# A four-layer convolution kernel: last layer with overlap-add, gelu and product moved ahead of the transposes, and border columns moved by DMA

## The chip, the cores and the metric

One core of a Trainium2 chip runs the whole program. The metric is the device time of one execution in microseconds. Names of engines are those of the profile: PE (TensorE matmul), PEld (its weight loads), DVE, ACT, POOL (GpSimd), and SP, whose queue issues DMAs.

## The reference

The input `x` is [4, 48, 256, 256], float32. Four residual layers follow, `x = x + conv_i(groupnorm(x))`. The change touches only the last one:

```
y = einsum('oc,bchw->bohw', w_in, x)                  # 48 -> 288 channels
f = rfft2(8x8 patches of y) * fft_mask;  y = irfft2(f)
y = depthwise 3x3 convolution of y, zero padding
x1, x2 = split(y, 2, axis=channels)                   # 144 and 144
out = einsum('oc,bchw->bohw', w_out, gelu(x1) * x2)   # 144 -> 48
```

## The kernel before, in words

The last layer is `stage_l3` (lines 2104 to 2548). It works on **slabs** of 8 image rows: 33 bands times 2 pairs of images, 66 slabs, numbered n. In a slab there are 64 patches of 8x8 pixels: 32 across, in two images. The 288 channels are handled in three groups j of 96, and u = 3n + j counts groups.

For each slab, PE does the following, and this order is written out by hand:

- `channels` (L2268): the 48 to 288 mixing, into `y` with 64 pixels on the partitions. ACT and DVE copy it out of PSUM (`read_y`, L2370) in 12 pieces.
- `convolve` (L2292), for each j: per channel one matmul of the 64 patches with a 64x100 matrix `d` that holds mask and 3x3 convolution together. It gives 10x10 outputs for each 8x8 patch: the outer ring belongs to the neighbouring patches. ACT and DVE copy the result to `turn` (`read_turn`, L2378) in five pieces each, with **patches on the partitions**.
- `transpose` (L2318): 50 transposes of 128x112, which put **channels on the partitions**. ACT (8) and DVE (5) copy them from PSUM to `spread` (L2403, L2391).
- On POOL, `join` (L2523, L2525) adds the columns that two neighbouring patches share; L2539 adds the bottom rows saved from the band above in `strip`; L2547 saves the new bottom rows. Neighbouring patches lie side by side in the free dimension of `spread`, so this is plain addition.
- `gelu` on ACT (L2415) and the product on DVE (`gated`, L2473), four pieces for each j; then `project` (L2333), 24 matmuls of 48x48 by 512 columns per slab on PE, and `residual` (L2482) on DVE.

SP loads `x` for the next slab (L2211, two of 48 partitions; L2213, two rows of ones with one partition each), stores the result (L2219) and loads the residual (L2228, eight). Another stage matters for the reading: L813 loads inputs of the first layer with 49 partitions each.

Semaphores order all this. Each engine works through its own list in order, so a wait holds up all that stands behind it.

Of the kernel before, what the change touches and what calls it, by code (L numbers as in the profile page):

```python
# [20 lines left out]
R = 8  # L21
# [48 lines left out]
def l3_channels():  # L70

    return [g * 3 * C + j * C + r * (C // 2) + i for r in range(2) for j in range(3) for g in range(2) for i in range(C // 2)]


def l3_place(pos):

    pair, x, parity = pos // 20, pos % 20 // 2, pos % 2
    return 2 * pair + parity, x
# [92 lines left out]
def lay_out(i):  # L171
# [79 lines left out]
    order = l3_channels()  # L251
    d["l3_win"] = np.ascontiguousarray(i["L3_conv_w_in"].T[:, order])
    real, pairs = _pairs()
    fm = i["L3_conv_fft_mask"].reshape(C6, 8, 5)[order]
# [8 lines left out]
    d["l3_dwb"] = np.repeat(np.ascontiguousarray(i["L3_conv_w_dw"].reshape(C6, 9)[order].T)[None], 64, axis=0)  # L263
    wout = np.zeros((HI + C, 3, C), np.float32)
    for s in range(2):
        wout[s * HI:s * HI + C] = i["L3_conv_w_out"].T.reshape(3, C, C).transpose(1, 0, 2)
    d["l3_wout"] = wout
# [1836 lines left out]
def stage_l3(nc, D, S):  # L2104
# [3 lines left out]
    BANDS = H // 8 + 1  # L2108
    CH = C // 2
# [7 lines left out]
    TILES = PPOS // 2  # L2117
    TS = 4
    TG = -(-TILES // TS)
    ON_DVE = (1, 4, 6, 9, 11)  # L2120
    TURNS = [[i for i in range(TG) if (i in ON_DVE) == bool(k)] for k in range(2)]
    E = [len(groups) for groups in TURNS]
    PAIRS = 5
    HN = 512
    LANES = HI + C
    with nc.cleanup_on_exit(), ExitStack() as ctx:
# [10 lines left out]
        turn = sb("turn", [128, PPOS, HI])  # L2137
        spread = sb("spread", [LANES, PAIRS, 10, 4, TX])
        strip = sb("strip", [LANES, 3, 8, 4 * TX])
        x = sb("x", [HI + C + 1, TX, PX])  # L2140
        gate, spare = sb("gate", [LANES, 3, 8 * W]), sb("spare", [LANES, 2 * HN])
        out = sb("out", [LANES, 2, 2, HN])
        win = spare[0:C, 0:C6]
        lt, wy = sb("lt", [C, 2, HI + C + 1]), sb("wy", [HI + C + 1, 2, C6])
        wout = sb("wout", [LANES, 3, C])
# [3 lines left out]
        MIX_SLOTS, CONV_SLOTS = (3, 2, 0, 1), (0, 1, 2, 0, 1)  # L2149
        consts, prep, wy_done, wy_out, cleared = (sem(n) for n in ("consts", "prep", "wy_done", "wy_out", "cleared"))  # L2150
        d_in = [sem(f"d_in{j}") for j in range(3)]
        x_loaded, res_loaded, stored = sem("x_loaded"), sem("res_loaded"), sem("stored")
        a_done, a_out, b_done, b_out = sem("a_done"), sem("a_out"), sem("b_done"), sem("b_out")
        e_done, e_out = [sem("e_done0"), sem("e_done1")], [sem("e_out0"), sem("e_out1")]
        f_done, f_out = [sem("f_done0"), sem("f_done1")], sem("f_out")
        joined, added, saved = sem("joined"), sem("added"), sem("saved")
        mixing, saving, blank = sem("mixing"), sem("saving"), sem("blank")
# [3 lines left out]
        def inner(pair):  # L2161

            return spread[:, pair, 1:9, :, :].rearrange("p x g t -> p x (g t)")

        def one_half(part, pair):

            return inner(pair)[:, :, part * 2 * TX:(part + 1) * 2 * TX]

        def turned(u, i):

            k = int(i in ON_DVE)
            return k, u * E[k] + TURNS[k].index(i) + 1

        def turned_up_to(u, i):

            return [u * E[k] + sum(g <= i for g in TURNS[k]) for k in range(2)]

        def pieces_of(i):

            return min((min(TS * i + TS, TILES) - 1) // 10 + 1, 4)  # L2180

        def flat_piece(n, j, piece):

            if j == 0 and piece >= 2 and n % 2 == 1:
                return spare[:, (piece - 2) * HN:(piece - 1) * HN]
            return gate[:, j, piece * HN:(piece + 1) * HN]

        def band_piece(n, j, piece):

            return flat_piece(n, j, piece).rearrange("p (x m) -> p x m", x=8)  # L2190

        def slabs(work):

            for q in range(2):
                for ty in range(BANDS):
                    n = q * BANDS + ty
                    work(q, ty, n, n == 0, n == 2 * BANDS - 1)

        @block.sync
        def _(sp):  # L2200
# [3 lines left out]
            def load_x(q, ty, n, first):  # L2204
# [3 lines left out]
                for s in range(2):  # L2208
                    at = B * NBLK if isinstance(ty, int) and ty == BANDS - 1 else ty + (q + 2 * s) * NBLK
# [5 lines left out]

            def store(n):
                sp.wait_ge(f_out, n * 4)
                for side in range(2):
                    sp.dma_start(D["out"][n - 1, side], out[side * HI:side * HI + C].rearrange("p s k n -> p (s k n)"))\  # L2219
                      .then_inc(stored, 16)  # L2220

            def load_residual(q, ty, n, first):
                if not first:
                    sp.wait_ge(stored, n * 32)
                for s in range(2):
                    for p in range(4):
                        src = D["x3"][q + 2 * s, :, ty * 8 + 2 * p:ty * 8 + 2 * p + 2, 1:W + 1]
                        sp.dma_start(out[p % 2 * HI:p % 2 * HI + C, :, p // 2, s * W:(s + 1) * W], src)\  # L2228
                          .then_inc(res_loaded, 16)
# [7 lines left out]
            def slab(q, ty, n, first, last):  # L2237
                if not last:
                    nq, nty = (1, 0) if q == 0 and isinstance(ty, int) and ty == BANDS - 1 else (q, ty + 1)
# [359 lines left out]
```

## Time and profile before

| | us |
|---|---|
| median of 3 runs (lowest, highest) | 12443.44 (12438.75, 12449.53) |
| span of the profiled execution | 12461.3 |
| of it, from the last layer's first convolution matmul to its last | 9449.7 to 12429.4 |
| PE busy, whole span | 12084.7 |

The profiled execution gives no other time of its own than its span, which is 0.14% above the median. A span runs from the first to the last instruction. Busy time of PE is that of overlapping matmuls. Windows and chain are given in microseconds from the start of the span.

### The profile page before, as it was taken

The page shows a single profiled execution, that of the slowest core. Times are in us where ns is not written, and L with a number is a line of the kernel's source. Part 1 is how long each engine was busy: PE and PEld are TensorE (multiplying, and loading weights), DVE is VectorE, ACT ScalarE, POOL GpSimd, SP SyncE. Part 2 cuts the span into 40 slices and gives each one's busy share as a digit, 9 for nine tenths or more (in the row PEclk, how much of TensorE's full clock was granted, in tenths as well). Part 3 has the DMA queues.
Part 4 walks back from the last instruction along what each step waited for, and adds up shares of the span by engine and source line. Part 5 has one row for each costly group of instructions (what it writes and reads, how often), then busy time and mean ns, then how long its engine had stood idle before and what let it go on. Part 6 is the DMA issues. An engine that isn't in the chain of part 4 may idle for free. (4 is left out here: it accounts for less than half of the span.)

```text
span 12461.3 us, 389987 instructions
## 1 busy us (share of the span) xinstructions
PE 12084.7 (97%) x160850; PEld 8648.5 (69%) x160850; DVE 7757.3 (62%) x17493; ACT 5633.1 (45%) x11858; POOL 4999.7 (40%) x4364
## 2 busy tenths in 40 slices
PE   8999999899989999899999999999998999999999
PEld 7877444499977777555555555555557888888887
DVE  0000455444435545788888888888887777777777
ACT  0000111243433333455555555555556777777776
POOL 0000222212420055566666666666663444444444
PEclk9999999999999999999999999999999999999999
DMA  4333465695984587766666666666662222222222
GB/s 142 132 132 132 127 159 154 147 179 89 166 164 146 147 230 199 93 88 87 88 89 88 88 88 88 88 88 87 89 87 67 57 57 57 57 54 56 55 55 52
DMA packets 2289545, 1323.30 MB, mean 106 GB/s; under 512 B 1876085, under 2 KB 2199164, under 8 KB 2202256
## 3 DMA queue, kind: packets, MB, share of 16 engines
q1 hardware_dynamic: 2013196, 1200.80, 49.5%
q10 hardware_dynamic: 275072, 105.14, 3.7%
q8 instruction: 843, 13.81, 0.5%
q14 instruction: 434, 3.55, 0.1%
HBM read 648.82 MB, written 450.45 MB: 88 GB/s over the span
## 5 line engine op out<-in xcount | busy, mean ns | idle before, releaser
L1803 PE MATMUL l_m<-l_wa,l_pix 128*128 128x288 f32 x8192 | 2211.4, 413 | 2.7 <-DVE l_wb L1985 2.7
L1803 PEld LDWEIGHTS l_m<-l_wa,l_pix 128*128 128x128 f32 x8192 | 1475.5, 190 | 688.8 <-issue 361.9
L1659 POOL TENSOR_TENSOR l_qkv<-l_qkv,l_copies 128x576 f32<-128x576 f32 x1024 | 1437.1, 1403 | 631.3 <-DVE l_qkv L1996 621.5
L1649 POOL TENSOR_TENSOR l_pix<-l_raw 128x516 f32<-128x516 f32 x1024 | 1217.1, 1189 | 1042.6 <-DVE l_t L2033 1017.1
L1484 PE MATMUL l1h_ps<-l1h_ring,l1h_w 96*96 96x256 f32 x6120 | 1328.8, 379 | 62.7 <-ACT l1h_ring L1426 60.2
L1484 PEld LDWEIGHTS l1h_ps<-l1h_ring,l1h_w 96*96 96x96 f32 x6120 | 999.8, 163 | 391.5 <-issue 60.4
L2318 PEld LDWEIGHTS l_e<-k_ident,l_turn 128*112 128x112 f32 x9900 | 1069.1, 133 | 173.0 <-issue 110.6
L2318 PE MATMUL l_e<-k_ident,l_turn 128*112 128x128 f32 x9900 | 1158.2, 275 | 11.4 <-ACT l_turn L2403 3.0
L2403 ACT ACTIVATE l_spread<-l_e 112x512 f32<-112x512 f32 (+1 forms) x1584 | 871.7, 569 | 521.4 <-PE l_e L2318 509.5
L1517 DVE SCALAR_TENSOR_TENSOR l1h_ring<-l1h_ps,l1h_bias,l1h_columns 96x256 f32<-96x256 f32 x1020 | 670.4, 657 | 678.4 <-PE l1h_ps L1484 672.7
L517 PE MATMUL l0a_rows<-l0a_x 128*49 128x245 f32 x8144 | 1043.0, 371 | 0.0
L878 PE MATMUL l0b_bank<-l0b_x,l0b_w 49*64 49x512 f32 x9216 | 1000.5, 592 | 4.4 <-DVE l0b_w L904 4.4
L2391 DVE COPY l_spread<-l_e 112x512 f32<-112x512 f32 x990 | 683.8, 691 | 354.8 <-PE l_e L2318 351.3
L1898 ACT ACTIVATE l_ks<-l_f 94x384 f32<-94x384 f32 x1024 | 497.9, 486 | 843.2 <-PE l_f L1818 843.2
L1818 PE MATMUL l_f<-l_qkv,l_a 64*94 64x384 f32 x4096 | 834.8, 483 | 1.6 <-POOL l_qkv L1659 1.5
L878 PEld LDWEIGHTS l0b_bank<-l0b_x,l0b_w 49*64 49x64 f32 x9216 | 431.1, 133 | 570.9 <-issue 570.9
L1809 PE MATMUL l_m<-l_wb,l_left 58*128 58x288 f32 x4096 | 774.5, 455 | 0.0
L1468 POOL TENSOR_TENSOR l1h_columns<-l1h_blocks,l1h_ring 96x2048 f32<-96x2048 f32 x63 | 350.7, 5588 | 1035.9 <-DVE l1h_ring L1517 1035.9
L2292 PE MATMUL l_a<-l_d,l_y 64*64 64x100 f32 x15048 | 741.3, 248 | 8.3 <-issue 7.2
L2292 PE MATMUL l_b<-l_d,l_y 64*64 64x100 f32 x15048 | 743.6, 248 | 3.7 <-issue 3.2
L1903 ACT ACTIVATE l_sd<-l_mv,l_eps 128x4 f32<-128x4 f32 x512 | 152.3, 297 | 1286.7 <-DVE l_mv L2016 1286.7
L1909 ACT ACTIVATE l_y<-l_i,l_shift,l_rsd 128x96 f32<-128x96 f32 x2048 | 709.3, 427 | 14.4 <-DVE l_shift L2023 0.4
(269 smaller groups left out, 22947.3 us busy)
## 6 DMA issues: line engine op xcount, KB each, us to landing
l0a_x<-x_px_dram SPq DMA_DIRECT2D x128, 1176.0 KB, 5.1
l0b_x<-x_in_dram SPq DMA_DIRECT2D x128, 493.8 KB
l_raw<-l_raw SPq DMA_DIRECT2D x128, 483.6 KB, 7.3
l_raw<-x_dram SPq DMA_DIRECT2D x1270, 48.0 KB, 3.7
l_x<-x3p_dram SPq DMA_DIRECT2D x132, 384.0 KB
l_out<-x_dram SPq DMA_DIRECT2D x528, 96.0 KB, 2.4
out_dram<-l_out SPq DMA_DIRECT2D x132, 384.0 KB, 4.5
x_dram<-l0b_out ACTq DMA_DIRECT2D x256, 193.5 KB, 3.1
```

The source lines that it names most:

```text
L517: last = nc.tensor.matmul(o[odd * ODD:odd * ODD + C1, lo:lo + n * C1], x[:, ks, ys, 2 + odd, :], x[:, k, y, e0 + odd:e0 + odd + n, :].rear ...
L878: last = nc.tensor.matmul(bank[2 * n + rt][h * HI:(h + 1) * HI, :], w[part, t, :], rows(part, k, 4 * n + h + t // 3 - rt)[:, :, t % 3:t % ...
L1484: last = nc.tensor.matmul(ps[g][0:C2, 0:GI * V], w[:, kernel, s, :], ring[:, g, before % DEEP, :, s:s + V], start=(s == 0), stop=(s == 2))
L1649: nc.gpsimd.tensor_tensor(pix[:, n % 2, i, half * HALF:(half + 1) * HALF].rearrange("p (r w) -> p r w", w=PW), in0, in1, op).then_inc(pix_ ...
L1659: nc.gpsimd.tensor_tensor(q, q, copies[:, g % 2, 1:2, :].broadcast_to([128, 2, OUTC]), ALU.add)\
L1803: last = nc.tensor.matmul(bank[i][:, 0:OUTC], pix[:, k, i, first:first + 128], wa[:, b, i, :], start=True, stop=(i in (1, 2)))
L1809: nc.tensor.matmul(bank[i][:, 0:OUTC], left[rows, k, first:first + 128], wb[rows, b, :], start=False, stop=True).then_inc(conv_done, 1)
L1818: last = nc.tensor.matmul(f[0:SLOTS, h, 0:2 * QK].rearrange("p (n o) -> p n o", n=2), a[k, 0:SLOTS], qkv[k, j % 4, 2 * r:2 * r + 2, 0:QK], ...
L1909: last = nc.scalar.activation(y[:, g, m, :], iv[:, m * C2:(m + 1) * C2], ACT.Identity, scale=rsd[:, g, m:m + 1], bias=shift[:, g, m:m + 1])
L2292: last = nc.tensor.matmul(bank[part * 64:(part + 1) * 64, i * PPOS:(i + 1) * PPOS], y[k, c, :], d[k, c, :], start=True, stop=True, skip_gr ...
L2318: last = nc.tensor.transpose(e[i % 4][0:LANES, at:at + 128], flat[:, q * 128:q * 128 + LANES], S["k_ident"][:])
L2403: return nc.scalar.activation(o, i, ACT.Copy)
```

## The change

Only `stage_l3`, and the layout of its constants and output, change.

- The channels are paired so that `x1` and `x2` of the same channel stand in the same partition of `turn`, which is now [128, 2 buffers, 10 x, 10 y, 2, 24]. The 128 partitions are two halves of channels, times two images, times 32 patches. Each group of 32 partitions is one row of patches.
- Columns that neighbouring patches share now lie on neighbouring partitions. `move_edges` on SP brings them together: eight DMAs for each j, from `turn` to `edge`, each of 31 partitions and 480 floats (1920 bytes) a partition. The edge add, the carry from `strip` and the saving of the strip then run on POOL with partitions as they are (960, 768 and 768 elements).
- Gelu and the product work on `turn` in two halves of 768 elements, before the transposes.
- The transposes take `gate`: 16 of 128x128 for each j instead of 50 of 128x112. ACT alone copies them out, four copies of 512 (`read_rows`) instead of 13 by ACT and DVE.
- The projection is 48 matmuls with 24 rows each, on four row groups of PE and into four banks, instead of 24 with 48 rows.
- The order on PE becomes: convolve 0, transpose 2 of the slab before, convolve 1, project the slab before, transpose 0, convolve 2, channels of the next slab, transpose 1. The residual comes in four loads instead of eight.

The core of the diff, lines added and kept:

```diff
+    return pos % 10, pos // 10
...
+        turn = sb("turn", [128, 2, 10, 10, 2, CH])
+        edge = sb("edge", [128, 2, 2, EDGE])
+        strip = sb("strip", [128, 3, 8, 2 * C])
...
+        gate = sb("gate", [128, 2, PX, LANE])
+        rows = sb("rows", [128, 3, GROUPS, 2, 2 * TX])
...
+        CONV_SLOTS = ((1, 2, 3, 1, 2), (1, 2, 0, 1, 0), (2, 3, 0, 1, 2))
+        TURN_SLOTS = ((1, 0), (3, 0), (0, 3))
...
+            def move_edges(n, j):
+
+                u = n * 3 + j
+                sp.wait_ge(a_out, conv_at(n, j, COMP))
+                sp.wait_ge(b_out, conv_at(n, j, COMP))
+                if u >= 2:
+                    sp.wait_ge(edged, u - 1)
+                for first in range(0, 128, TX):
+                    here, there = slice(first, first + TX - 1), slice(first + 1, first + TX)
+                    for side, column, dst, src in ((0, 9, there, here), (1, 0, here, there)):
+                        sp.dma_start(edge[dst, u % 2, side, :],
+                                     turn[src, u % 2, column].rearrange("p y g i -> p (y g i)")).then_inc(edge_in[u % 2], 16)
...
             def slab(q, ty, n, first, last):
                 if not last:
+                    load_x(*((1, 0) if q == 0 and ty == BANDS - 1 else (q, ty + 1)), n + 1, False)
+                move_edges(n, 0)
+                move_edges(n, 1)
                 if not first:
+                    store(n - 1)
+                move_edges(n, 2)
...
+            def transpose(n, j, ended):
+
                 u = n * 3 + j
+                for i, bank in enumerate(turn_banks(j)):
+                    if j == 0 and i % 2 == 0:
+                        bank_pair_read(conv_at(n, 1, 4 + i // 2))
+                    elif j == 1 and i % 2 == 0:
+                        bank_pair_read(conv_at(n, 2, 2 + i // 2) if ended else (n + 1) * AB + 9 + i // 2)
+                    elif j == 2 and i == 0 and ended:
+                        pe.wait_ge(t_out, u * 4)
+                    elif j == 2 and i == 2 and not ended:
+                        bank_pair_read(conv_at(n + 1, 0, 3))
+                    if i % 2 == 0:
+                        pe.wait_ge(gate_out, u * 2 + 1 + i // 2)
+                    for k in range(4):
+                        group = 4 * i + k
+                        last = nc.tensor.transpose(bank[:, k * 128:(k + 1) * 128],
+                                                   gate[:, u % 2, 4 * group:4 * group + 4, :].rearrange("p m i -> p (m i)"),
                                                    S["k_ident"][:])
+                    last.then_inc(t_done, 1)
...
+            def project(n, ended):
+
+                pe.wait_ge(t_out, n * 12 + 12)
+                bank_pair_read(conv_at(n, 2, 5) if ended else conv_at(n + 1, 1, 2))
+                for k in range(6):
+                    j, r = k // 2, k % 2
+                    for m in range(4):
+                        lanes = slice(m * LANE, m * LANE + CH)
+                        for side in range(2):
+                            last = nc.tensor.matmul(e[m][side * HI:side * HI + C, :], wout[lanes, j, r, :],
+                                                    rows[lanes, j, side * 8:(side + 1) * 8, r, :], start=(k == 0), stop=(k == 5),
                                                     skip_group_check=True)
+                        if k == 5:
+                            last.then_inc(p_done, 1)
...
+                    if j == 0 and not first:
+                        transpose(n - 1, 2, False)
+                    if j == 1:
+                        if not first:
+                            project(n - 1, False)
+                        transpose(n, 0, False)
+                if not last:
+                    channels(1 if q == 0 and ty == BANDS - 1 else q, n + 1, False)
+                transpose(n, 1, last)
...
+            if g == 0 and u >= 2:
+                eng.wait_ge(gate_out, 2 * u - 2)
+                eng.wait_ge(saved, u - 1)
+            eng.wait_ge(done, conv_at(n, j, g) + 1)
+            places = turn[:, u % 2].rearrange("p x y g i -> p (x y) g i")
+            copy(places[:, :, part, CSTARTS[g]:CSTARTS[g] + CSIZES[g]],
+                 slots[CONV_SLOTS[j][g]][part][:, 0:CSIZES[g] * PPOS].rearrange("p (c t) -> p t c", t=PPOS)).then_inc(ready, 1)
...
+            def gelu(u, h):
+
+                if h == 0:
+                    act.wait_ge(edged, u + 1)
+                    act.wait_ge(carried, u + 1)
+                nc.scalar.activation(half(u, 0, h), half(u, 0, h), ACT.Gelu).then_inc(gelu_out, 1)
+
+            def read_rows(n, j):
 
                 u = n * 3 + j
+                if j == 0 and n > 0:
+                    act.wait_ge(p_done, n * 4)
+                for i, bank in enumerate(turn_banks(j)):
+                    act.wait_ge(t_done, u * 4 + i + 1)
+                    copy(rows[:, j, 4 * i:4 * i + 4].rearrange("p q r t -> p (q r t)"), bank[:]).then_inc(t_out, 1)
...
+                u = n * 3
+                for g in range(COMP):
+                    read_turn(act, copy, 0, n, 0, g, a_done, a_out)
+                    if g in (0, 2) and not first:
+                        gelu(u - 1, g // 2)
+                if not first:
+                    read_rows(n - 1, 2)
+                for g in range(COMP):
+                    read_turn(act, copy, 0, n, 1, g, a_done, a_out)
+                for h in range(2):
+                    gelu(u, h)
+                read_rows(n, 0)
+                for g in range(COMP):
+                    read_turn(act, copy, 0, n, 2, g, a_done, a_out)
+                if last:
+                    for h in range(2):
+                        gelu(u + 1, h)
+                else:
+                    for g in range(YR):
+                        read_y(act, copy, 0, n + 1, g, False, a_done, b_done, a_out)
+                        if g in (3, 6):
+                            gelu(u + 1, g // 6)
+                read_rows(n, 1)
...
+            def gated(u, h):
+
+                dve.wait_ge(gelu_out, u * 2 + h + 1)
+                if u >= 2:
+                    dve.wait_ge(t_done, u * 4 - 6 + 2 * h)
+                nc.vector.tensor_tensor(gated_half(u, h), half(u, 0, h), half(u, 1, h), ALU.mult).then_inc(gate_out, 1)
+
+            def residual(n, m):
+
+                dve.wait_ge(p_done, n * 4 + m + 1)
+                if m == 0:
+                    dve.wait_ge(res_loaded, n * 64 + 64)
+                o = out[:].rearrange("p y s (t x m) -> p y x (s t) m", x=2, m=4)[:, :, :, :, m]
+                nc.vector.tensor_tensor(o, e[m][0:HI + C, :].rearrange("p (y x t) -> p y x t", y=4, x=2), o, ALU.add)\
...
+                for g in range(COMP):
+                    read_turn(dve, nc.vector.tensor_copy, 1, n, 0, g, b_done, b_out)
+                    if g in (1, 3) and not first:
+                        gated(u - 1, g // 2)
+                for g in range(COMP):
+                    read_turn(dve, nc.vector.tensor_copy, 1, n, 1, g, b_done, b_out)
+                for h in range(2):
+                    gated(u, h)
+                if not first:
+                    for m in range(4):
+                        residual(n - 1, m)
+                for g in range(COMP):
+                    read_turn(dve, nc.vector.tensor_copy, 1, n, 2, g, b_done, b_out)
+                if last:
+                    for h in range(2):
+                        gated(u + 1, h)
+                else:
+                    for g in range(YR):
+                        read_y(dve, nc.vector.tensor_copy, 1, n + 1, g, False, b_done, a_done, b_out)
+                        if g in (4, 7):
+                            gated(u + 1, g // 7)
...
+                    tile = turn[:, u % 2].rearrange("p x y g i -> p x (y g i)")
+                    pool.wait_ge(a_out, conv_at(n, j, COMP))
+                    pool.wait_ge(b_out, conv_at(n, j, COMP))
+                    pool.wait_ge(edge_in[u % 2], 128 * (u // 2) + 128)
+                    nc.gpsimd.tensor_tensor(tile[:, 1:9:7], tile[:, 1:9:7], edge[:, u % 2], ALU.add).then_inc(edged, 1)
+                    pool.wait_ge(edged, u + 1)
                     if ty == 0:
+                        pool.sem_inc(carried, 1)
                     else:
                         pool.wait_ge(saved, u - 2)
+                        nc.gpsimd.tensor_tensor(tile[:, 1:9, 0:2 * C], tile[:, 1:9, 0:2 * C], strip[:, j], ALU.add)\
+                            .then_inc(carried, 1)
+                    pool.wait_ge(carried, u + 1)
+                    pool.sem_inc(mixing, 1)
+                    nc.gpsimd.tensor_copy(strip[:, j], tile[:, 1:9, 8 * C:10 * C]).then_inc(saved, 1)
```

## Rows read from the trace of the kernel before

**Rows 1.** The page: busy time by engine, and the granted clock in 40 slices.
```profile
PE 12084.7 (97%) x160850; PEld 8648.5 (69%) x160850; DVE 7757.3 (62%) x17493; ACT 5633.1 (45%) x11858; POOL 4999.7 (40%) x4364
...
PEclk9999999999999999999999999999999999999999
```

**Rows 2.** One line, L2292: its matmuls' min/median/max, first and last start.
```profile
L2292 PE MATMUL l_a<-l_d,l_y x15048: 242/246/426, 9449.7 to 12429.4; 64*64 64x100 f32 x198
```

**Rows 3.** Window of steady slabs: us; PE, PEld, DVE, ACT, POOL busy; clock, DMA share, GB/s.
```profile
9900.00:12400.00 2500.00, 2441.47 (x56770) 2123.42 (x56762) 1959.21 (x3198) 1867.11 (x3476) 1065.15 (x990) 1.00 0.25 56
```

**Rows 4.** Chain of work inside one slab: start us, us, what.
```profile
11001.40 5.74 PE l_e L2318 x50
...
11011.61 2.60 PE l_e L2333 x21
...
11020.27 0.23 PE l_a L2292
...
11024.55 1.47 PE l_e L2268 x48
...
11032.85 5.60 PE l_e L2318 x50
```

**Rows 5.** Groups by line and shape, last stage: count, busy us, mean ns, idle before.
```profile
L2318 PE MATMUL l_e<-k_ident,l_turn 128*112 128x128 f32 x9900 | 1158.2, 275 | 11.4 <-ACT l_turn L2403 3.0 <-DVE l_turn L2378 0.8 <-ACT l_y L2403 0.3
...
L2403 ACT ACTIVATE l_spread<-l_e 112x512 f32<-112x512 f32 x1386 | 796.0, 596 | 509.5 <-PE l_e L2318 508.8 <-issue 0.5
...
L2473 DVE TENSOR_TENSOR l_gate<-l_gate,l_spread 112x512 f32<-112x512 f32 x726 | 474.0, 684 | 4.1 <-ACT l_gate L2415 3.4
L2539 POOL TENSOR_TENSOR l_spread<-l_spread,l_strip 112x1024 f32<-112x1024 f32 x192 | 453.6, 2363 | 15.1
L2415 ACT ACTIVATE l_gate<-l_spread 112x512 f32<-112x512 f32 x726 | 421.2, 625 | 2.0 <-POOL l_spread L2525 1.1 <-POOL l_spread L2539 0.9
L2378 DVE COPY l_turn<-l_b 128x500 f32<-128x500 f32 x594 | 402.9, 678 | 135.6 <-PE l_b L2292 120.1
L2403 ACT ACTIVATE l_turn<-l_a 128x500 f32<-128x500 f32 x594 | 392.4, 661 | 149.9 <-PE l_a L2292 132.0
```

**Rows 6.** Waits of the last stage: engine and line, for whom, us, times, longest.
```profile
ACT l_spread L2403 <- PE l_e L2318: 509.5, 986, 2.5
```

**Rows 7.** The DMA-issuing queue SP through one slab: start us, us, line, count.
```profile
11021.09 4.57 SPq L2228 DMA_DIRECT2D l_out<-x_dram  x8
11032.93 0.31 SPq L2211 DMA_DIRECT2D l_x<-x3p_dram  x1
...
11078.00 0.31 SPq L2211 DMA_DIRECT2D l_x<-x3p_dram  x1
```

**Rows 8.** DMA view, 11033 to 11040 us: packets, and what was issued.
```profile
DMA packets 135, 0.84 MB, mean 121 GB/s; under 512 B 34, under 2 KB 34, under 8 KB 34
...
q1 hardware_dynamic: 132, 0.80, 57.9%
...
l_x<-x3p_dram SPq DMA_DIRECT2D x2, 384.0 KB
l_x<-k_ones_dram SPq DMA_DIRECT2D x2, 8.0 KB
```

**Rows 9.** SP's issues, 1338 to 1345 us, where loads have 49 partitions.
```profile
1338.20 1.98 SPq L813 DMA_DIRECT2D l0b_x<-x_in_dram  x4
```

**Rows 10.** DMA view, 1338 to 1345 us.
```profile
DMA packets 97, 0.93 MB, mean 132 GB/s; under 512 B 7, under 2 KB 7, under 8 KB 7
```

**Rows 11.** Windows: loads with 49 partitions; 1 KB loads; 1 KB copies within SBUF.
```profile
1342.00:1344.00 2.00, 2.00 (x11) 2.00 (x11) 0.00 (x0) 0.00 (x0) 0.06 (x1) 0.50 0.46 175
11022.00:11024.00 2.00, 2.00 (x104) 2.00 (x100) 1.74 (x4) 1.91 (x5) 1.13 (x2) 1.00 0.78 199
8200.40:8202.40 2.00, 2.00 (x14) 1.29 (x14) 1.09 (x5) 1.35 (x4) 0.44 (x2) 1.00 0.82 174
```

**Rows 12.** Line L2228: from issue to landing.
```profile
DMA to landing us min/median/max: 2.0/2.4/11.3
```

More of the change, by code:

```diff
@@ L262, in lay_out @@
     d["l3_m"] = m
[L263 to L267, printed above, removed]
+    d["l3_dwb"] = np.repeat(np.ascontiguousarray(i["L3_conv_w_dw"].reshape(C6, 9).T)[None], 64, axis=0)
+    wout = np.zeros((4, 32, 3, 2, C), np.float32)
+    wout[:, 0:C // 2] = i["L3_conv_w_out"].T.reshape(3, 2, C // 2, C).transpose(2, 0, 1, 3)
+    d["l3_wout"] = wout.reshape(128, 3, 2, C)
     return d
@@ L2116, in stage_l3 @@
     AB = YR + 3 * COMP
[L2117 to L2125, printed above, removed]
+    EDGE = 10 * C
+    LANE = 32
+    GROUPS = PX // 4
     with nc.cleanup_on_exit(), ExitStack() as ctx:
@@ L2351, in slab @@
                     convolve(n, j)
-                    if j < 2 and not first:
-                        project(n, j)
-                    if j == 2 and not last:
-                        nq = 1 if q == 0 and isinstance(ty, int) and ty == BANDS - 1 else q
-                        channels(nq, n + 1, False)
-                    transpose(n, j, first)
-            slabs(slab)
-            for part in range(2):
-                project(2 * BANDS, part)
-        def read_y(eng, copy, s, n, first, done, other, ready, between):
-            for g, size in enumerate(SIZES):
-                if g == 0 and not first:
-                    eng.wait_ge(other, n * AB)
-                eng.wait_ge(done, n * AB + (g + 1))
-                bank = slots[MIX_SLOTS[g % 4]][s]
-                m0 = s * TX + STARTS[g]
-                copy(y[:, :, m0:m0 + size], bank[:, 0:size * C3].rearrange("p (t c) -> p c t", c=C3)).then_inc(ready, 1)
-                between(g)
@@ new lines, in slab, with read_y @@
+                transpose(n, 1, last)
+            slabs(slab)
+            transpose(N - 1, 2, True)
+            project(N - 1, True)
+        def read_y(eng, copy, s, n, g, first, done, other, ready):
+            if g == 0 and not first:
+                eng.wait_ge(other, n * AB)
+            eng.wait_ge(done, n * AB + (g + 1))
+            bank = slots[MIX_SLOTS[g % 4]][s]
+            m0 = s * TX + STARTS[g]
+            copy(y[:, :, m0:m0 + SIZES[g]], bank[:, 0:SIZES[g] * C3].rearrange("p (t c) -> p c t", c=C3)).then_inc(ready, 1)
@@ L2476, in residual @@
-            def residual(n, part, s):
-                dve.wait_ge(f_done[s], n * 2 + (part - 1))
-                if part == 0 and s == 0:
-                    dve.wait_ge(res_loaded, n * 128)
-                o = out[:, s, part, :].rearrange("p (m x) -> p m x", x=8)
-                nc.vector.tensor_tensor(o, e[2 + s][0:LANES, :].rearrange("p (x m) -> p m x", x=8), o, ALU.add)\
+            dve.wait_ge(blank, 1)
+            dve.sem_inc(blank, 1)
+            for g in range(YR):
+                read_y(dve, nc.vector.tensor_copy, 1, 0, g, True, b_done, a_done, b_out)
```

308 lines of the change are left out of this document (85 added, 223 removed).

## The prediction, made before the changed kernel ran

> **What bounds the kernel now.** I began with the page: PE is busy 97% of the span at full clock [rows 1]. Then I took the last layer alone. The convolution line runs from 9449.7 to 12429.4 us [rows 2], so 66 slabs take 45.2 us each, and SP's loads repeat at the same pace, 11032.93 and 11078.00 [rows 7]. In steady slabs PE is busy 2441 of 2500 us, DVE 1959, ACT 1867, POOL 1065, and the DMA engines 25% at 56 GB/s [rows 3]. The chain of work says who ends last: it is PE's list, one piece after another [rows 4]. ACT stands idle 509.5 us in this stage for transposes [rows 6]. So a slab is bound by PE, and its pieces can be read off the chain: one convolution of a group 4.3 us (11020.27 to 11024.55), the channels 8.3 (to 11032.85), one set of 50 transposes 5.75, half a projection 2.6 [rows 4]. Together 3 x 4.3 + 8.3 + 3 x 5.75 + 2 x 2.6 = 43.6 us, with 1.6 us of waits.
>
> **PE after the change.** A transpose costs 5.75 / 50 = 0.115 us. 48 in place of 150 take 5.5 us and save 11.7. The wider tile (128 columns for 112) streams the same 128 columns, so I keep 0.115. Convolutions and channels keep their count. The projection doubles to 48 matmuls of half the rows. Before, 24 matmuls (48 instructions, since float32 takes two each) took 5.2 us, so four ran at once at 0.43 us a round [rows 4]. No row shows row groups of 32 at work. The bounds are eight at once (5.2 us) and one at a time (96 x 0.43 = 41 us). The nearest row ran four tiles at once on separate parts of the array. I take 5.2, and 10.4 for four at once is covered by what follows. PE needs 12.9 + 8.3 + 5.5 + 5.2 = 31.9 us a slab.
>
> **ACT, DVE, POOL.** ACT loses its copies to `spread` (8 of each 13) and takes 12 copies of 512 at 0.6 us; gelu in 6 pieces of 768 elements, scaled from 625 ns for 512 [rows 5], is 0.9 us each. In sum about 28 us. DVE loses its share of the 13 copies and makes 6 products of 768 elements, 1.0 us each by 684 ns for 512 [rows 5]; about 25 us. POOL's two-input add costs 2363 / 1024 = 2.3 ns an element [rows 5]: edge add (960) 2.2 us, carry (768) 1.8 us, and saving under 1 us, three times, about 15 us. None of them would bound the slab; all that is removed from them is hidden either way.
>
> **What is added: the border columns.** This is the part on which the time hangs. `move_edges` issues 8 DMAs for each group, 24 a slab, on SP. SP's issues take 0.3 to 0.57 us each [rows 7], so 3 to 5 us for a group. That is bearable. The question is how fast the data moves. Each DMA has 31 partitions of 1920 bytes.
>
> The packet counts say how a DMA is spread. From 11033 to 11040 us SP issued two DMAs of 48 partitions and two of one. The queue shows 132 packets: 34 small ones, and 98 others, one for each partition. The 34 are completions: 2 x 16 + 2 x 1 [rows 8]. So 48 partitions go to 16 engines, and one partition to one engine. With 49 partitions, four loads were queued within 2 us [rows 9]; the one that finished by 1345 us left 7 completions [rows 10]. While all four were pending the DMA engines were busy 0.46 of 16, thus about seven, at 175 GB/s [rows 11]. Two things follow. 49 partitions did not go to 16 engines but to 7, which divides 49, as 16 divides 48. And four loads in flight together did not fill other engines: they sat **on the same seven**. 31 has no divisor but 1 and itself. So each of the 8 DMAs should run on one engine, and all on the same one, one after another.
>
> The Trainium skill, "DMA: Bandwidth & Descriptors", section "Why a DMA increments its semaphore by 16 and not by 1", says so: the largest number up to 16 that divides both sides' outermost dimension, 127 partitions giving 1, and the lowest-numbered engines. By that rule the sum is the one below; by sixteen engines it would be that of the first rival.
>
> What one engine gives: 175 / 7 = 25 GB/s for packets of 10 KB. With 1 KB packets on all engines it was 199 / (0.78 x 16) = 16 GB/s, and for copies within SBUF 174 / (0.82 x 16) = 13 GB/s [rows 11]. 59.5 KB therefore take between 2.4 and 4.5 us. I take **2.55 us**, near the low end, because a lone engine has no fifteen others to contend with. A group's 8 DMAs take 20.4 us on that engine (bounds 19 and 36), a slab's 24 take 61.2. The store of 96 rows of 8 KB gives this engine 6 packets at 25 GB/s, 2.0 us, and it is queued in between.
>
> **Can the engine be kept busy all the time?** Two buffers of `turn` let group 1 be queued while group 0 moves, and group 2 is ready in time: after group 0 lands come POOL 4.0, gelu 1.8, product 1.0, residual 2.7, convolve and read 4.5, 14 us, under 20. But ACT and DVE work in order. At the start of a slab they read piece 0 of group 0, then stop for the gelu of the last slab's group 2, and only then read the rest, for which `move_edges` waits. So once a slab the engine runs dry. From landing to next packet: POOL 2.2 + 1.8, gelu 0.9, two reads 1.4, gelu 0.9, product 1.0, last read 0.6, and the fixed part of a DMA 1.9 (2.4 us to landing less the transfer itself [rows 12]): 10.8 us. The loads of `x` and of the residual pass in this gap and cost nothing. PE's 31.9 us lie beside the DMAs. At 1.2 GHz, as granted at 1342 us [rows 11], they would be 64 us and still mostly beside them.
>
> **Sum.** 61.2 + 2.0 + 10.8 = 74.0 us a slab against 45.2: 28.8 x 66 = 1901 us more. The profiled execution's span of 12461 would become 14362; it stands 18 us (0.14%) above the median of the runs, so the median is 12443 + 1901 = **14345 us**. Setup (three more fills on DVE, a few us) and the tail are under 30 us together.
>
> **Rivals.**
>
> *The columns spread over the engines.* If the 31 partitions were dealt out unevenly over 16 engines, or successive DMAs took different engines, a group's columns would arrive 5 to 6.5 us after its last read. Then PE bounds the slab again. Its waits: after convolve 0, gelu of group 0 can start after reads 2.3, DMAs 6, POOL 4.0, about 12.5 us; PE has convolve 1, projection and transposes (11.4 us) for that, then waits for gelu and product, and convolve 2 waits for two residual adds. About 5 us of waits give 37 us a slab, 8.2 x 66 = 541 us less: **11,900 us**, faster. Against it: 49 partitions went to seven engines and stayed there [rows 10, 11]. The point that decides: with 2.0 + 10.8 us beside it, the slab is even at (45.2 - 12.8) / 3 = 10.8 us a group, 1.35 us a DMA, which two engines would give. Chance 0.12.
>
> *The engine is one, and slow.* If 1920-byte copies within SBUF go at 13 to 16 GB/s as in [rows 11], a group takes 30 to 36 us and a slab 103 to 121: 16,200 to 17,400 us. For it: those are the rows with the nearest packet size. Against: sixteen engines shared the ports there. Chance 0.06.
>
> *The projection goes one matmul at a time.* 41 us instead of 5.2. It stands ahead of transpose 0 and thus of convolve 2, whose columns come 14 us late for the idle engine: 88 us a slab, 15,300 us. Against: four tiles ran at once before [rows 4]. Chance 0.04. The Trainium skill, "TensorEngine Tiling (Array Packing)", section "Tiling Modes", lists 32x64 as eight tiles; no run here shows it.
>
> **How the numbers follow.** One engine at 2.3 to 3.3 us a DMA, the forecast, holds 0.78: 68 to 92 us a slab, 13,900 to 15,500 us. The slower cases bring 0.10 and the spread case 0.12. Range 13,600 to 15,900: this takes in the forecast with a faster engine (2.2 us, 66 us a slab) and the projection's case, and leaves out the spread case and the slowest engine. A measurement of this kernel tells about 0.2% from no change. All cases but the spread one are slower: slower 0.87, faster 0.12; for "within 0.2%" a DMA would have to take 1.35 us exactly: 0.01.
>
> **What the changed kernel's profile would show.** Right: DMA share near 1/16 plus the loads, about 0.15, in the last layer; 24 issues of 60 KB a slab that land 20 us and more after their issue; POOL's edge add waiting for them; completions of one packet a DMA; PE busy under half. Wrong: completions of 16 a DMA, landing in 2 to 4 us, PE above 80%. If the slab is longer and the transposes' and projection's matmuls stand close together, the time of one DMA is what I mis-sized; if the projection's row is far above 5 us, it is the row groups. If the engine turns out to have no gap, the once-a-slab stop costs less than 10.8 us.

## The result, and the profile after

The changed kernel takes **14431.67 us** (median of 4 runs, 14429.67 to 14436.68) against 12446.49 us (4 runs): ratio 1.160, 95% interval 1.158 to 1.161. The forecast was 14345 us. The difference of 1985 us (1974 between the spans of the profiled executions) lies in the last layer. From the first to the last start of the convolution line (9454.2 to 14380.1), divided by 66 as in [rows 2], a slab takes 4925.9 / 66 = 74.6 us, where 74.0 was forecast; that is 29.5 us a slab more than before, 1946 us in all. The work behind the last convolution is 23 us longer, and the first one starts 4.5 us later. Slab lengths below are all taken that way.

The page of the changed kernel (busy time, granted clock, and the head of the chain that ended last) answers to [rows 1]:

```profile
PE 11788.2 (82%) x157286; PEld 8331.2 (58%) x157286; DVE 7087.2 (49%) x16108; ACT 5164.2 (36%) x10670; POOL 4680.8 (32%) x3770
...
PEclk9999999999999999999999999977777777777777
...
DMA 14%; SPq 9%; POOL 4%; PE 3%; DVE 3%; issue 1%; ACT 1%; POOLq 0%; ACTq 0%; DVEq 0%
```

PE is no longer what ends the stage: the chain runs through the DMAs and SP's queue. Steady slabs, with the columns of [rows 3] (PE, PEld, DVE, ACT, POOL busy; clock, DMA share, GB/s):

```profile
9900.00:14200.00 4300.00, 2279.59 (x55681) 1922.52 (x55681) 1446.51 (x2114) 1518.06 (x2574) 826.63 (x513) 0.74 0.20 52
```

PE is busy 53% of the time, at a mean clock of 0.74. The waits of the stage name what comes last (engine and line, for whom: total us, times, longest):

```profile
POOL l_turn L2518 <- DMA l_edge<-l_turn: 3768.8, 182, 60.5
DVE l_gate L2469 <- ACT l_turn L2394: 2564.0, 197, 21.2
ACT l_turn L2394 <- POOL l_turn L2524: 2457.7, 192, 19.7
...
PE l_a L2318 <- DVE l_gate L2469: 1081.3, 67, 20.7
```

They are one wait handed on: POOL waits for the columns, ACT's gelu for POOL, DVE's product for the gelu, and PE's transposes for the product. How the columns travel is seen in 10 us with little else to move. The DMA view and the window of the same stretch:

```profile
DMA packets 118, 0.26 MB, mean 26 GB/s; under 512 B 5, under 2 KB 112, under 8 KB 112
```
```profile
11530.00:11540.00 10.00, 6.99 (x171) 6.43 (x164) 5.91 (x11) 5.48 (x11) 4.86 (x3) 0.86 0.07 26
```

112 packets are under 2 KB, 5 of them completions: 107 carry columns, which is 3.5 DMAs of 31. The other six are five rows of the store and one of PE's or another engine's instructions. All together move at 26 GB/s and with a DMA share of 0.07, just over 1/16: one engine, always busy. The 5 completions fit one for each DMA that ends, four for the columns and one for this engine's part of the store. Eight DMAs at 26 GB/s take 8 x 59.5 / 26 = 18.3 us. The edge adds of POOL, each of which waits for the eight DMAs of its group, show how long they take (the first three are those of groups 0, 1 and 2 of one slab, the last that of group 0 of the next):

```profile
11511.57 2.20 POOL L2518 TENSOR_TENSOR l_turn<-l_turn,l_edge 128x960 f32<-128x960 f32 x1 [25.37 <-DMA l_edge<-l_turn]
...
11530.60 2.23 POOL L2518 TENSOR_TENSOR l_turn<-l_turn,l_edge 128x960 f32<-128x960 f32 x1 [13.96 <-DMA l_edge<-l_turn]
...
11556.62 2.20 POOL L2518 TENSOR_TENSOR l_turn<-l_turn,l_edge 128x960 f32<-128x960 f32 x1 [20.91 <-DMA l_edge<-l_turn]
...
11587.38 2.20 POOL L2518 TENSOR_TENSOR l_turn<-l_turn,l_edge 128x960 f32<-128x960 f32 x1 [25.69 <-DMA l_edge<-l_turn]
```

The three distances are 19.0, 26.0 and 30.8 us here, and 19.1, 25.8 and 30.4 us as means of 60 slabs. The first is that of eight DMAs with nothing between. SP's issues of these DMAs (count, min/median/max ns):

```profile
L2201 SPq DMA_DIRECT2D l_edge<-l_turn x1584: 561/2222/3446, 9462.2 to 14393.4; - x198
```

In the median an issue holds SP for 2.2 us, about as long as one of these DMAs takes to move. The first three or four of a group whose queue is empty take 0.56 to 0.60 us, the later ones wait: SP is held back by its own queue. The once-a-slab stop can be followed through the engines' timelines (start us, us, engine, what; in brackets the idle time before and who ended it):

```profile
11556.62 2.20 POOL L2518 TENSOR_TENSOR l_turn<-l_turn,l_edge 128x960 f32<-128x960 f32 x1 [20.91 <-DMA l_edge<-l_turn]
11558.90 1.80 POOL L2524 TENSOR_TENSOR l_turn<-l_turn,l_strip 128x768 f32<-128x768 f32 x1
...
11560.79 0.84 ACT L2394 ACTIVATE l_turn<-l_turn 128x768 f32<-128x768 f32 x1 [14.85 <-POOL l_turn L2524]
11561.54 1.18 ACT L2387 ACTIVATE l_turn<-l_e 128x500 f32<-128x500 f32 x2
11562.59 0.84 ACT L2394 ACTIVATE l_turn<-l_turn 128x768 f32<-128x768 f32 x1
...
11563.72 0.95 DVE L2469 TENSOR_TENSOR l_gate<-l_turn 128x768 f32<-128x768 f32 x1
11564.58 0.57 DVE L2381 COPY l_turn<-l_e 128x400 f32<-128x400 f32 x1
...
11565.53 29.85 SPq L2201 DMA_DIRECT2D l_edge<-l_turn  x16
```
```profile
11562.00:11564.00 2.00, 1.75 (x33) 1.52 (x34) 2.00 (x4) 2.00 (x5) 0.00 (x0) 0.50 0.00 0
```

The columns of the last slab's group 2 land at 11556.6. From there POOL, gelu, reads, gelu, product, last read follow one another, and SP issues again at 11565.5. In between no column moves: until 11560.7 the engine passes its part of the loads of the residual and of `x` (48 packets of 1 KB and 8 of 8 KB), and then nothing (second fence, share 0.00 at 0 GB/s). Then the groups that stand for the steps of the forecast, by shape (count, busy us, mean ns, idle before; as in [rows 5]):

```profile
L2518 POOL TENSOR_TENSOR l_turn<-l_turn,l_edge 128x960 f32<-128x960 f32 x198 | 438.0, 2212 | 3993.8 <-DMA l_edge<-l_turn 3768.8 <-DVE l_y L2371 167.9 <-ACT l_y L2387 57.1
L2469 DVE TENSOR_TENSOR l_gate<-l_turn 128x768 f32<-128x768 f32 x396 | 372.3, 954 | 2564.0 <-ACT l_turn L2394 2564.0
L2332 PE MATMUL l_e<-l_rows,l_wout 24*48 24x512 f32 x6336 | 356.8, 590 | 0.7 <-ACT l_rows L2387 0.7
L2394 ACT ACTIVATE l_turn<-l_turn 128x768 f32<-128x768 f32 x396 | 325.9, 839 | 2509.9 <-POOL l_turn L2524 2457.7 <-POOLq L2521 52.2
L2477 DVE TENSOR_TENSOR l_out<-l_e,l_out 112x512 f32<-112x512 f32 x264 | 269.1, 1094 | 9.0 <-PE l_e L2332 9.0
```

The projection's busy time is 356.8 / 66 = 5.4 us a slab.

### The profile page after: what moved, and what is told of

Read it like the earlier page. It is cut to its first block and busy times, and to the rows that moved or that the text cites. A ratio compares the mean times of both kernels' runs of the same rounds, so it can differ in the third digit from the quotient of the medians.

```text
span 14434.9 us, 377731 instructions
## 1 busy us (share of the span) xinstructions
PE 11788.2 (82%) x157286; PEld 8331.2 (58%) x157286; DVE 7087.2 (49%) x16108; ACT 5164.2 (36%) x10670; POOL 4680.8 (32%) x3770
## 5 line engine op out<-in xcount | busy, mean ns | idle before, releaser
L2518 POOL TENSOR_TENSOR l_turn<-l_turn,l_edge 128x960 f32<-128x960 f32 x198 | 438.0, 2212 | 3993.8 <-DMA l_edge<-l_turn 3768.8
L2469 DVE TENSOR_TENSOR l_gate<-l_turn 128x768 f32<-128x768 f32 x396 | 372.3, 954 | 2564.0 <-ACT l_turn L2394 2564.0
L2296 PE MATMUL l_e<-l_d,l_y 64*64 64x100 f32 x17424 | 524.1, 272 | 994.8 <-ACT l_turn L2387 973.6
L2394 ACT ACTIVATE l_turn<-l_turn 128x768 f32<-128x768 f32 x396 | 325.9, 839 | 2509.9 <-POOL l_turn L2524 2457.7
L2318 PE MATMUL l_a<-k_ident,l_gate 128*128 128x128 f32 x1056 | 265.9, 402 | 1081.3 <-DVE l_gate L2469 1081.3
L2296 PEld LDWEIGHTS l_e<-l_d,l_y 64*64 64x64 f32 x17424 | 459.7, 150 | 1036.4 <-ACT l_turn L2387 986.3
L2318 PEld LDWEIGHTS l_a<-k_ident,l_gate 128*128 128x128 f32 x1056 | 194.8, 211 | 1153.5 <-issue 1153.5
```

The lines of the kernel that those rows point to most:

```text
L2296: last = nc.tensor.matmul(bank[part * 64:(part + 1) * 64, i * PPOS:(i + 1) * PPOS], y[rows_of, c, :], d[rows_of, c, :], start=True, stop=True,
L2318: last = nc.tensor.transpose(bank[:, k * 128:(k + 1) * 128], gate[:, u % 2, 4 * group:4 * group + 4, :].rearrange("p m i -> p (m i)"), S[" ...
L2518: nc.gpsimd.tensor_tensor(tile[:, 1:9:7], tile[:, 1:9:7], edge[:, u % 2], ALU.add).then_inc(edged, 1)
```

## The experiments

Theory A is that of the forecast: a DMA of 31 partitions runs on one engine, always the same, and the slab is 24 of them, the store and the stop. Its rivals are that the size or the number of the copies is what costs, whatever engines they use, or that another part of the change (POOL, the projection, the slower clock) sets the time. A kernel for which no range is given was executed once. Each batch had the kernel before beside it, with medians of 12453.78, 12461.86 and 12449.19 us.

**Two DMAs for each one** (16 + 15 partitions; nothing left out):

```
-  here, there = slice(first, first + TX - 1), ...
+  for low, count in ((0, 16), (16, 15)):
+      here, there = slice(first + low, first + low + count), ...
```

> Each DMA of 31 partitions is cut into one of 16 and one of 15: same bytes, same result, 48 DMAs a slab instead of 24. One engine for a partition count without divisors (A): 16 and 15 partitions use 16 and 15 engines, the columns arrive some 6 us after the last read, the slab falls from 75 to 37-40 us, 11,900 to 12,100 us. Rival: SP's issuing of so many DMAs is what takes the time (B): with twice as many the slab grows, above 15,000 us. Rival: copies within SBUF are slow by their bytes, on however many engines (C): no change, 14,400.

Measured 13078.34 us (13066.25 to 13080.94), ratio to before 1.050 (1.048 to 1.051), slab 54.2 us. Twice the DMAs for the same bytes, and 1353 us less: it is the spread over engines, not count or bytes, that held the changed kernel. But the time stands 1000 us above what A gave, and SP's queue shows a large part of why (issues of the columns):

```profile
L2203 SPq DMA_DIRECT2D l_edge<-l_turn x3168: 538/816/2059, 9468.3 to 13047.1; - x198
```

The issues with 16 partitions take 0.56 to 0.60 us, those with 15 take 0.82 to 0.85. With what SP waits for in them, 48 a slab hold it for 36.6 us, and the residual's loads and the others stand behind them.

**One partition fewer, two fewer, and about half.** In the three kernels the slice is 30, 29 or 17 partitions in place of 31; the columns of the partitions left over are not moved:

```
-  here, there = slice(first, first + TX - 1), slice(first + 1, first + TX)
+  here, there = slice(first, first + 30), slice(first + 1, first + 31)
```

> Each DMA moves 30 of its 31 partitions (the seam between the last two patches of a row is left out). A: 30 divides into 15 engines, 11,850 to 12,050 us. B and C: 14,300 to 14,432, since 3% of the bytes are gone.

> 29 of 31 partitions (two seams left out), 29 has no divisor. A: still one engine, 24 x 2 packets of 0.078 us less a slab, 3.7 us x 66 = 250 us less than the changed kernel, about 14,190. C: like the run with 30. If any count below 31 spreads: 11,900.

> 17 of 31 partitions (14 seams of each row left out), one engine by A: 24 x 14 packets less, 26 us a slab, 48.5 us, about 12,700 us; the stop once a slab stays. If the time of one DMA were fixed and not by packet (rival D): 14,400.

Measured: 30 partitions 12586.40 us (slab 46.8), 29 partitions 14187.55 (71.0), 17 partitions 13164.14 (55.5). One partition fewer takes away 1845 us, and one fewer again gives 1601 back. No rival by size does that. 30 has the divisor 15; 29 has none. From 31 to 29 the kernel loses 244 us, or 3.7 us a slab, for 48 packets less: 77 ns a packet, 25 GB/s, the rate of [rows 11]. The DMA view of 30 partitions, over the 7 us in which eight are issued:

```profile
DMA packets 310, 0.49 MB, mean 70 GB/s; under 512 B 101, under 2 KB 298, under 8 KB 298
...
l_edge<-l_turn SPq DMA_DIRECT2D x8, 56.2 KB
```

101 small packets, where there was one for each DMA: 15 each for seven DMAs make 105, so 30 partitions go to fifteen engines. Two times of A are missed. With 30 partitions it gave 12,050 us at most and 12,586 came; what holds that kernel is the subject of the next runs. With 17 it gave 12,700. A slab has 24 DMAs of 17 x 0.077 = 1.3 us, 31.4 us, so 24.1 us are left where I had put 12.8 for store and stop. The edge adds of that kernel lie 10.4, 23.3 and 22.2 us apart. So the stop that came once a slab now comes twice, 17.7 us without columns together: group 1's columns are through before group 2's are ready.

**Four DMAs for each eight** (112 + 15 partitions across the patch rows; at three seams a group the wrong neighbour's column is added):

```
-  for first in range(0, 128, TX):
+  for low, count in ((0, 112), (112, 15)):
```

> Four DMAs a group instead of eight: 112 and 15 partitions for each side (16 and 15 engines). The six patches at the seams between rows of patches get a column of the wrong row; everything else is as in the changed kernel. The runs with 30 partitions and with 16 + 15 left a slab of 47 and 55 us instead of the 37 I had put down for spread columns. Theory: SP's issuing, 0.87 us a DMA, is the next limit: four issues less a group, 3.5 us off the chain from last read to gelu, 42 to 44 us a slab, 12,250 to 12,400. Rival: the rest of the slab (half clock, instruction fetch) is what holds it: 47 us, 12,590.

Measured 12402.98 us, slab 44.2: 2.6 us a slab under 30 partitions, for 12 issues fewer, at the edge of the forecast 42 to 44. It is faster than before (12461.86 beside it), by half a per cent.

**No columns at all** (SP moves none; POOL adds what the buffer holds):

> No border columns are moved (POOL adds zeros): leaves out the DMAs and their wait, all else in place. It gives the floor of the rest. Theory: last read to POOL's add took 9.1 us with 30 partitions; without it 37 to 40 us a slab, 11,900 to 12,100. Rival: if PE is stalled by something else (fetch of its instructions behind the loads of x and of the residual), 42 or more, above 12,200.

Measured 12228.93 us, slab 41.5, above the theory's range and at the rival's. My first rival had put the slab *with* spread columns at 37 us. Even without any of them it is 4.5 us longer, so something beside the columns was missing from that price. Nor is this time the floor that I took it for: a kernel further down moves the columns and is faster.

**Reads of the next group ahead of gelu and product** on ACT and DVE (nothing left out; both buffers serve):

```
-  if g in (0, 2) and not first:
-      gelu(u - 1, g // 2)
   if not first:
+      for h in range(2):
+          gelu(u - 1, h)
```

> The changed kernel, but ACT and DVE finish reading group 0 before they do gelu and product of the slab before, so the next columns can be queued before the last have landed. One engine with a stop once a slab (A): the 10.6 us in which the queue is dry go, the loads of x and of the residual (5 us of that engine) no longer hide in it: 68 to 70 us a slab, 13,950 to 14,100. If the stop is not what empties the queue: 14,432.

Measured 14006.69 us, slab 68.1: 425 us off, 6.4 us a slab, as expected. It is the stop, and most of it goes when group 0's copies no longer wait for the gelu of the slab before: of the three distances between edge adds only the third, which holds the stop, fell, from 30.4 to 23.7 us. POOL's wait for the DMAs fell with it (the waits of this kernel):

```profile
POOL l_turn L2519 <- DMA l_edge<-l_turn: 3304.9, 180, 61.1
```

**Merged, seams made zero, x loaded later.** This version leaves nothing out. POOL multiplies both sides of `edge` by a column that is 0 at the seams, and SP issues the loads of `x` behind the columns of group 0:

```
+  move_edges(n, 0)
   if not last:
       load_x(...)
-  move_edges(n, 0)
...
+  nc.gpsimd.tensor_scalar(edge[:, u % 2, side], edge[:, u % 2, side], seam[:, side:side + 1], None, ALU.mult)
```

> As the run with four DMAs, made right: POOL multiplies the moved columns by 0 at the seams (two one-input operations of 480 elements, 1.0 us a group), and the load of x stands behind the columns of group 0 instead of right behind the load of the residual, so that the two do not fill the DMA engines together. If SP's issuing and the fetch of PE's instructions behind those loads are the two limits: 38 to 41 us a slab, 12,050 to 12,200, faster than both kernels. If the load's place does nothing: 43 to 45, 12,330 to 12,450.

Measured 12346.41 us (12344.10 to 12360.01), ratio 0.991 (0.990 to 0.993), slab 43.3. Faster than both kernels, yet short of what I expected. The number lies where "the load's place does nothing" had put it, but the reason is another, the price of the mask:

```profile
L2525 POOL TENSOR_SCALAR l_edge<-l_edge,l_seam x396: 1476/1483/3084, 9463.5 to 12312.0; 128x480 f32<-128x480 f32 x198
```

1.48 us for 480 elements in the median and 1.68 in the mean, three times what I had assumed, twice in each group and ahead of the edge add. The next kernel differs from this one by the mask alone and has a slab of 40.0 us: the mask costs 3.3 us a slab.

**The load of x alone** (the kernel with four DMAs a group, and only `load_x` put behind group 0's columns; the seams as there):

> The run with four DMAs a group, with only the load of x put behind the columns of group 0 (columns at the seams as wrong as there). If PE's idle time without a releaser in the convolutions (some 4 us a slab there) is its instructions waiting behind the joined loads of the residual and of x: about half of it goes, 2 us a slab, 12,250 to 12,300 against 12,403. If those gaps have another cause: 12,380 to 12,420.

Measured 12126.95 us, slab 40.0: 4.2 us a slab less than with the load ahead, 2.6% under before, and below the range I gave. A load put later, which nobody waited for, was worth more than all 12 saved issues. The kernel is even 1.5 us a slab faster than the one without columns, in which the load of `x` still stands ahead. Where the gain came from is seen best in the kernel with 30 partitions. SP there issues the residual's loads and those of `x` back to back:

```profile
11510.76 2.12 SPq L2216 DMA_DIRECT2D l_out<-x_dram  x4
11512.98 0.38 SPq L2186 DMA_DIRECT2D l_x<-x3p_dram  x1
```
```profile
11515.00:11518.00 3.00, 2.25 (x108) 2.06 (x96) 1.75 (x3) 2.09 (x4) 2.46 (x2) 1.00 1.10 204
11518.00:11521.00 3.00, 0.00 (x0) 0.00 (x0) 1.15 (x2) 1.36 (x3) 0.00 (x0) 0.79 0.69 126
11521.00:11524.00 3.00, 1.05 (x24) 1.05 (x28) 0.00 (x0) 0.00 (x0) 0.00 (x0) 0.50 0.01 3
```
```profile
11522.95 0.42 PE L2296 MATMUL l_a<-l_d,l_y 64*64 64x100 f32 x1 [5.70 <-issue]
```

The DMA engines are full, and PE stops for 5.7 us in the middle of a convolution, "issue": no semaphore, no operand. It goes on at half the clock. The same wait in the kernel with four DMAs a group, and in this one, from 9900 to 12100 us:

```profile
PE l_e L2296 <- issue: 106.5, 37, 5.2
...
PE l_b L2296 <- issue: 31.0, 16, 5.0
...
PE l_a L2296 <- issue: 28.3, 15, 3.4
```
```profile
PE l_e L2296 <- issue: 33.8, 40, 2.4
...
PE l_b L2296 <- issue: 9.2, 21, 0.9
PE l_a L2296 <- issue: 7.5, 14, 1.4
```

165.8 us in 50 slabs became 50.5 us in 55: 2.4 us a slab less. The mean clock rose from 0.93 to 0.97. PE's busy time in these windows went from 36.1 to 34.7 us a slab and its idle time from 8.1 to 5.3, which is the whole 4.2. The columns themselves didn't come sooner: from SP's first issue of a group to the edge add it took 5.6, 5.3 and 5.7 us with the load ahead, and 5.8, 7.0 and 5.7 with it behind.

What arrives late is PE's own instructions. The page has a DMA queue of kind "instruction", whose packets have 16 KB. In the kernel with 30 partitions, the DMA view has none of them from 11511 to 11520 us, while the loads fill the engines, and one from 11520 to 11522:

```profile
q1 hardware_dynamic: 996, 1.63, 94.2%
```
```profile
q1 hardware_dynamic: 16, 0.02, 6.6%
q8 instruction: 1, 0.02, 4.8%
```

It ended at 11521.64, and PE went on at 11522.95. After 9900 us this kernel has 59 stops of over 1.5 us for "issue" ahead of a convolution matmul, and every one of them ended 1.2 to 1.8 us after such a packet; a moment taken at random lies there in 10% of cases. With four DMAs a group it was 52 of 52 stops, and with the load of `x` behind the columns only three stops were left. That the two loads together delay these packets is shown by that last number; how they share the DMA engines is not.

**The residual's layout alone** (no columns, as above; the residual is added in the order of `out`'s memory, so that sums stand in other places):

```
-  o = out[:].rearrange("p y s (t x m) -> p y x (s t) m", x=2, m=4)[:, :, :, :, m]
+  o = out[:, m].rearrange("p s w -> p (s w)")
```

> The run without border columns, and the residual add reads and writes its tiles straight through instead of with a stride of 8 floats (sums land in the wrong places of the output, same number of elements). Theory: the stride makes each of the four adds 1.09 us instead of 0.69, and they stand between the projection and the last convolution of a slab: 1.6 us a slab less, 12,120 against 12,229. If they are hidden: 12,229.

Measured 12111.79 us, slab 39.6, 1.9 us less, as expected. The residual's group in the kernel without columns and in this one, each from 9900 to 12100 us:

```profile
L2470 DVE TENSOR_TENSOR l_out<-l_e,l_out 112x512 f32<-112x512 f32 x208 | 212.1, 1088 | 0.0
```
```profile
L2470 DVE TENSOR_TENSOR l_out<-l_e,l_out 112x512 f32<-112x512 f32 x220 | 135.9, 675 | 0.0
```

**The mask on DVE** in place of POOL (nothing left out):

> The mended kernel, with the seam columns multiplied by 0 on DVE instead of POOL. On POOL these two operations took 2.9 us or more a group, where 1.0 was expected, on the path from the columns' landing to gelu. Theory: 2 to 3 us a slab less than mended, 12,150 to 12,230. Rival: DVE then waits for the columns with its other work behind it and gives it back: 12,350 or more.

Measured 12328.28 us (12323.83 to 12331.25), ratio 0.990 (0.988 to 0.992), slab 42.9: short of the expectation again, and not told apart from the version with the mask on POOL (0.991 of the kernel before beside it). DVE does each multiply in 0.46 us and not in 1.48, but the wait moved with the work. The waits from 9900 to 12200 us:

```profile
POOL l_turn L2536 <- DVE l_edge L2474: 1363.9, 143, 14.2
```

DVE takes the mask in its own order, behind products, residual adds and reads, and POOL waits for that instead.

## Why the prediction was right, and where it was not

**What bounds the kernel now, and PE after.** Right in substance: PE no longer sets the end, and POOL, gelu and product took 2.2, 0.84 and 0.95 us for 2.2, 0.9 and 1.0. PE was busy 53% and not under half, and the DMA share was 0.20 and not 0.15; the mean clock fell to 0.74. PE was busy for 39.5 us a slab where I had 31.9; the largest miss is the transposes, 9.6 us for 5.5, at the lower clock. The forecast had said that half clock would be hidden mostly, and since the waits are for the columns, it was. The projection took 5.4 us a slab against 5.2 for twice the matmuls. Of the rivals, "one matmul at a time" falls by that row.

**The border columns.** Right in mechanism and size, and shown: 29, 30 and 31 partitions tell the divisor from the size. The time of one DMA was put at 2.55 us; 31 packets of 77 ns give 2.4, and eight of them 19.1 where I had 20.4. The slow engine of the third case (30 to 36 us a group) falls: a lone engine moves packets of 1920 bytes at 26 GB/s, as fast as those of 10 KB.

**The loads beside the columns.** Wrong, and the sum is as close as it is partly by luck. I wrote that the loads of `x` and of the residual pass in the gap and cost nothing. The one engine's own part of them does. But SP issues them while group 2's columns still move, and while their packets pass on the other fifteen engines, the columns on this one go slower (so the timing says; no run isolates it). The DMA engines are then busy 0.73:

```profile
11544.00:11554.00 10.00, 3.70 (x161) 3.50 (x160) 1.36 (x2) 1.28 (x2) 0.00 (x0) 0.84 0.73 157
```

From SP's first load to the landing of group 2, the column packets follow one another every 0.11 us on average and not every 0.077, which adds 4.8 us a slab; the store's six packets take 1.9 us, for the 2.0 of the forecast. From edge add to edge add the slab was put together from 20.4 + 22.4 + 31.2 = 74.0 us, and it is 19.1 + 25.8 + 30.4, about 75.2, in its steady part (74.6 over all 66 slabs). The 4.0 us that I paid too much for 24 DMAs hid the 4.8 that I had at nothing.

**The once-a-slab stop.** Forecast 10.8 us from landing to next packet. The timeline gives 8.9 us from landing (11556.6) to SP's next issue (11565.5). From the last packet of one slab's columns to the first of the next it is 10.8 us there, and 10.5 as a mean of 60 slabs. That the copies' place in ACT's and DVE's order is its cause is shown by 6.4 us a slab that came off when the order was changed.

**SP's issues.** I took 0.3 to 0.57 us from loads. Where nothing holds SP up, an issue of 31 partitions takes 0.56 to 0.60 us, so this was right for the changed kernel. But its queue fills, and then an issue takes 2.2 us; that lies beside the one engine's work. It is not so for every copy: with 15 or 30 partitions an issue takes 0.78 to 0.85 us, and in the kernel with 48 DMAs issuing is most of the slab.

**DVE's residual.** Not in my sum. I priced it at the old 686 ns; with its new order of elements it takes 1094 ns. Its four pieces take 4.1 us in a row where I had 2.7. In the changed kernel it lies beside the DMAs of group 1; with the columns out of the way the strided order costs 1.9 us a slab.

**The rival "spread over the engines"** had the right condition and the wrong price: 11,900 us, 37 us a slab, where 30 partitions give 46.8. The runs account for 8.7 of the 9.8 us between: 2.6 by fewer issues, 4.2 by the place of the load of `x` (which together give the 40.0 measured), and 1.9 for the residual, if it adds to the others, which no run shows. My walk through PE's waits had free instructions and full clock in it. So the break-even of 1.35 us a DMA was too generous as well: with 17 partitions, 1.3 us each, the slab is 55.5 us and not 45.2. Spreading by 15 + 16 or by 30 was still slower than before. By these runs the rival's condition would not have been enough for "faster"; the number of issues and the place of a load had to change as well. The chance of 0.12 rested on a price that was too low.

**What stays open:** what a mask without the price of either engine would bring. 12,127 us, without one, is the lowest time seen with the columns moved, and it has the strided residual in it. A product fused into the edge add wasn't tried. Of the 4.2 us that the load's place was worth, 2.4 are stops in the convolutions; how much of the remainder follows from those stops through the lower clock behind them is not settled. Nor is why an issue of 15 or 30 partitions is dearer than one of 16, 17, 31 or 112.

## What to carry to other kernels

Look at the partition count of every DMA before anything else: 30 against 31 partitions was 13% of the whole kernel's time, and merging slices, even over seams that must be mended later, beats splitting them, since each issue costs its queue 0.6 to 0.8 us. Read a queue of DMAs as a list with an order: a load that is early enough anyway should stand behind the small transfers that others wait for, and not next to another large load. And when a wait is removed by moving work to another engine, read that engine's order first; the wait is likely to move with it.

## What the runs showed of the hardware that I had not expected

- Issuing a copy within SBUF holds SP for 0.55 to 0.60 us with 16, 17, 31 or 112 partitions and for 0.78 to 0.85 us with 15 or 30; behind a full queue it holds SP for as long as a whole DMA, 2.2 us median and up to 3.4.
- PE can stop for 5.7 us "for issue" (8.3 at most in the kernel with 30 partitions) while two large groups of loads (0.8 and 0.8 MB) run back to back on all DMA engines, and come back at half clock. In the convolutions it went on 1.2 to 1.8 us after a packet of the instruction queue, in all 111 stops over 1.5 us of the two kernels looked at.
- A copy that runs on one DMA engine goes slower while loads pass on the others: 0.11 us from packet to packet instead of 0.077.
- An add on DVE of 512 elements from PSUM and SBUF takes 675 ns with contiguous operands and 1.09 us where the SBUF side is strided.
- GpSimd's multiply by one value for each partition takes 1.48 us for 480 elements, 3.1 ns each (DVE 0.46 us); its add of two tensors takes 2.3 ns, its copy 1.07 ns (0.82 us for 768).
